# Input stages of a four-block pair-map kernel: every tile in four equal rounds, transposes first, longer leads

## The reference

```python
xn = layer_norm(x_gn)                                  # over the 64 channels of a token
left  = (xn @ Wl + bl) * sigmoid(xn @ Wlg + blg)       # block 3: times the mask too
right = (xn @ Wr + br) * sigmoid(xn @ Wrg + brg)
gate  = sigmoid(xn @ Wg + bg)
out   = einsum('kjd,kid->ijd', left, right)            # over a token axis, per channel
x     = x + (layer_norm(out) @ Wo + bo) * gate
```

## Time and profile before

| | |
|---|---|
| runs | 1729.84, 1731.24, 1733.73 us |
| profiled execution | 1738.9 us, span 1737.1 us |
| input stage of block 0 | about 51 to 223 us from the span's start |
| of block 1 | about 433 to 603 us |
| of block 3 | about 1357 to 1552 us |
| PE, DVE, ACT, POOL busy over the span | 74%, 78%, 66%, 55% |
| granted PE clock, mean | 0.916 of full speed |

### The profile page before, as it was taken

The page is one execution under the profiler, slowest core; times in us unless marked ns, Lnnn a source line. Parts: engine busy times, 40 slices in busy tenths (PEclk is TensorE's granted clock), DMA queues, the critical chain, the costliest instruction groups (busy, mean ns, idle before and its releaser), DMA issues.

```text
span 1737.1 us, 30472 instructions
## 1 busy us (share of the span) xinstructions
PE 1292.9 (74%) x9640; PEld 788.4 (45%) x9640; DVE 1361.7 (78%) x3807; ACT 1146.5 (66%) x2644; POOL 953.0 (55%) x663
## 2 busy tenths in 40 slices
PE   0588878998688887987999466677666577769665
PEld 0233366654333476654876133333334233338654
DVE  6888724997888616987999899999997777751688
ACT  0588824995788715985343577777774488851698
POOL 0799702875999504874555034444445787820454
PEclk9999998999899998998999569988998799999679
DMA  7244363776455454774443144544445334443477
GB/s 262 79 118 120 92 150 89 223 213 168 98 119 122 92 134 125 229 202 121 109 111 87 22 92 100 118 99 105 115 98 134 91 98 108 100 103 93 160 241 254
DMA packets 408784, 225.51 MB, mean 130 GB/s; under 512 B 343408, under 2 KB 343728, under 8 KB 408624
## 3 DMA queue, kind: packets, MB, share of 16 engines
q1 hardware_dynamic: 270192, 185.81, 39.3%
q10 hardware_dynamic: 138432, 37.76, 9.3%
HBM read 114.97 MB, written 66.06 MB: 104 GB/s over the span
## 4 chain that ended last, share of the span: by engine, by line
issue 29%; POOL 21%; DVE 20%; ACT 17%; PE 12%; DMA 2%; SPq 0%; POOLq 0%; ACTq 0%; DVEq 0%
ACT work L1045 12%; POOL ln_s L507 6%; DVE stats L760 5%; POOL work L499 5%; POOL work L513 4%; PE ps L1165 4%; PE ps L1282 4%; POOL work L477 3%; POOL pairs L545 2%; PE ps L1194 2%; DVE pairs L818 2%; ACT work L1058 2%; DVE stats L844 2%; ACT work L1027 1%; DVE pairs L891 1%
## 5 line engine op out<-in xcount | busy, mean ns | idle before, releaser
L507 POOL TENSOR_TENSOR ln_s<-ln_s,half_power 128x8 f32<-128x8 f32 x216 | 356.5, 1650 | 285.9 <-DVE ln_s L769 230.2
L1207 PE MATMUL ps<-wfold,work 64*128 64x320 f32 x1728 | 341.0, 486 | 100.1 <-DVE pairs L818 52.5
L1045 ACT ACTIVATE work<-work,ln_s 128x64 f32<-128x64 f32 x576 | 212.3, 429 | 116.6 <-DVE ln_s L776 116.5
L1165 PE MATMUL ps<-work,ones 128*128 128x512 f32 x432 | 241.4, 672 | 47.6 <-ACT work L1015 46.6
L1045 ACT ACTIVATE work<-pairs,ln_s 128x64 f32<-128x64 f32 x648 | 262.4, 488 | 18.9 <-DVE ln_s L776 18.9
L1207 PEld LDWEIGHTS ps<-wfold,work 64*128 64x128 f32 x1728 | 137.9, 188 | 271.9 <-DVE pairs L818 133.3
L818 DVE TENSOR_TENSOR pairs<-ps,work 128x256 f32<-128x256 f32 x288 | 169.0, 597 | 63.4 <-ACT work L1058 58.4
L1058 ACT ACTIVATE work<-ps 128x384 f32<-128x384 f32 x432 | 194.6, 476 | 4.8 <-PE ps L1207 3.8
L1194 PE MATMUL ps<-ident,work 128*128 128x128 f32 x864 | 149.1, 300 | 46.3 <-DVE work L787 26.4
L1027 ACT ACTIVATE work<-ps 128x512 f32<-128x512 f32 x216 | 128.4, 594 | 73.3 <-PE ps L1194 71.9
L1105 ACT ACTIVATE pairs<-pairs,rescale 128x256 f32<-128x256 f32 x288 | 122.4, 497 | 70.7 <-DVE work L949 70.7
(11 more groups left out here) (153 smaller groups left out, 2482.5 us busy)
## 6 DMA issues: line engine op xcount, KB each, us to landing
work<-x_mid SPq DMA_DIRECT2D x144, 256.0 KB, 2.8
gate_dram<-work ACTq DMA_DIRECT2D x108, 256.0 KB, 2.8
work<-gate_dram SPq DMA_DIRECT2D x108, 256.0 KB, 3.1
work<-in_x_in SPq DMA_DIRECT2D x72, 256.0 KB, 2.8
work<-x_nat SPq DMA_DIRECT2D x144, 128.0 KB, 2.9
x_mid<-work SPq DMA_DIRECT2D x72, 256.0 KB, 2.6
pairs<-in_x_in SPq DMA_DIRECT2D x4, 2304.0 KB, 19.3
work<-pairs SPq DMA_DIRECT2D x96, 96.0 KB, 3.0
```

The lines of the kernel that those rows point to most:

```text
L507: pool.tensor_tensor(ln_s[:, b, RSTD, :], ln_s[:, b, VAR, :], half_power[:, 0:U], ALU.pow)\
L1045: last = act.activation(dst[:, r % dst.shape[1], u * C:(u + 1) * C], src, ACT.Identity, scale=ln_s[:, b, RSTD, u:u + 1], bias=ln_s[:, b, S ...
L1165: last = pe.matmul(ps[:, bank, :], ones[:], src[:, b, :], start=first, stop=end, skip_group_check=True)
L1207: last = pe.matmul(ps[:, PAIR_BANKS[n % 3] + odd, 0:PROJ], xnT[rows, b, pair * P:(pair + 1) * P], wfold[rows, q, 0:PROJ], start=True, stop ...
```

## The change

It touches the lists of the input stages, the buffers that longer leads need, and the indices that follow from them:

- **PE** transposes tile t+1 ahead of the four projections of tile t, not between the second and the third.
- **ACT** evacuates t+1 first, then gate 0, the DMA issue, and its tokens in three parts instead of two halves, each between two gates. In blocks 0 and 1 the parts have 1, 2 and 2 tokens, in block 3 2, 2 and 2.
- **DVE** starts with shift t+2 and variance t+3, then two moments of t+4 (before: t+3), store 0, two moments, store 1, the first token of t+2, store 2, the other tokens (2, in block 3 one), store 3.
- **POOL** scales t+5 and centres t+6 (before t+4 and t+5); the power stays at t+3.
- `normed` holds six tiles, `stats` and `ln_s` hold four; the waits that guard them look as much farther back. These waits are shared with the output stages. Input and output stages get a transposed buffer each (`xnT_in`, `xnT_out`) at other addresses.
- Block 3 reads the mask straight from `mask_sb`: the copy L808 and its wait are gone, 36 of each.
- In block 0's multiplication, DVE waits for the gate stores before it writes `fold_ein`.

```diff
+NORM_RING = 6
-        normed = part(work, 1024, ROW, RING)
+        xin, normed = part(work, 0, ROW), part(work, 1024, ROW, NORM_RING)
+        xn, xnT_in = (part(work, 4096 + 1024 * k, ROW) for k in range(2))
-        stats = sb("stats", [P, 2, PAIRS, 6])
-        ln_s = sb("ln_s", [P, 2, 3, U])
+        stats = sb("stats", [P, RING, PAIRS, 6])
+        ln_s = sb("ln_s", [P, RING, 3, U])
...
 # POOL, centre
-                wait_free(pool, xn_ready, tr_base(l, 0) + t - 3)
-                wait_free(pool, xn_act, tr_base(l, 0) + t - 3)
+                if t >= NORM_RING:
+                    pool.wait_ge(xn_ready, tr_base(l, 0) + t - NORM_RING + 1)
+                    pool.wait_ge(xn_act, tr_base(l, 0) + t - NORM_RING + 1)
...
 # POOL, token_rstd (xn_ready too), and DVE, ln_shift
-                wait_free(pool, xn_act, n - 1)
+                wait_free(pool, xn_act, n - 3)
...
-                    pipeline(pool, [(4, lambda t, b, r: scale(l, t, b, r), RING),
-                                    (5, lambda t, b, r: centre(l, t, b, r), RING),
+                    pipeline(pool, [(5, lambda t, b: scale(l, t, b)),
+                                    (6, lambda t, b: centre(l, t, b)),
                                     (3, lambda t, b: token_rstd(l, 0, t, b))])
...
 # DVE, store_pair
-                if l == 3 and pair == 0:
-                    dve.tensor_copy(mask_t[:, b, :], mask_sb[:, cols(t)]).then_inc(mask_ready, 1)
-                    dve.wait_ge(mask_ready, t + 1)
...
-                    pipeline(dve, [(3, lambda t, b, r: ln_moments(l, 0, t, b, r), RING),
-                                   (0, lambda t, b: store_pair(l, 0, t, b)),
-                                   (2, lambda t, b: ln_shift(l, 0, t, b)),
-                                   (3, lambda t, b: ln_var(l, 0, t, b)),
-                                   (0, lambda t, b: store_pair(l, 1, t, b)),
-                                   (2, lambda t, b, r: normalise(l, 0, xn, t, b, r), RING),
-                                   (0, lambda t, b: store_pair(l, 2, t, b)),
-                                   (0, lambda t, b: store_pair(l, 3, t, b))])
+                    moments = lambda which: (4, lambda t, b, r: ln_moments(l, 0, t, b, r, which), RING)
+                    scaled_tokens = lambda part_: (2, lambda t, b, r: normalise(l, 0, xn, t, b, r, part_), RING)
+                    store = lambda pair: (0, lambda t, b: store_pair(l, pair, t, b))
+                    pipeline(dve, [(2, lambda t, b: ln_shift(l, 0, t, b)), (3, lambda t, b: ln_var(l, 0, t, b)),
+                                   moments((0, 1)), store(0),
+                                   moments((2, 3)), store(1),
+                                   scaled_tokens(0), store(2),
+                                   scaled_tokens(1), store(3)])
...
-                    pipeline(act, [(0, lambda t, b: gates(q, 0, t, b)),
-                                   (-1, lambda t, b: store_gate(q, t, b)),
-                                   (1, lambda t, b: evacuate_xnT(tr_base(l, 0) + t, t, b, proj_ready, PAIRS * (TILES * q + t - 1))),
-                                   (0, lambda t, b: gates(q, 1, t, b)),
-                                   (2, lambda t, b, r: normalise(l, 0, xn, xn_transposed(0), t, b, r, HALF_ONE), RING),
-                                   (0, lambda t, b: gates(q, 2, t, b)),
-                                   (2, lambda t, b, r: normalise(l, 0, xn, xn_transposed(0), t, b, r, HALF_TWO), RING),
-                                   (0, lambda t, b: gates(q, 3, t, b))])
+                    third = lambda k: (2, lambda t, b, r: normalise(l, 0, xn, xn_transposed(0), t, b, r, k, 3), RING)
+                    gate_of = lambda pair: (0, lambda t, b: gates(q, pair, t, b))
+                    pipeline(act, [(1, lambda t, b: evacuate_xnT(xnT_in, tr_base(l, 0) + t, t, b, proj_ready, PAIRS * (TILES * q + t - 1))),
+                                   gate_of(0), (-1, lambda t, b: store_gate(q, t, b)),
+                                   third(0), gate_of(1),
+                                   third(1), gate_of(2),
+                                   third(2), gate_of(3)])
...
-                    pipeline(pe, [(0, lambda t, b: project(l, 0, t, b)),
-                                  (0, lambda t, b: project(l, 1, t, b)),
-                                  (1, lambda t, b, r: transpose_xn(l, 0, t, b, r), RING),
-                                  (0, lambda t, b: project(l, 2, t, b)),
-                                  (0, lambda t, b: project(l, 3, t, b))])
+                    projected = lambda pair: (0, lambda t, b: project(l, pair, t, b))
+                    pipeline(pe, [(1, lambda t, b, r: transpose_xn(l, 0, t, b, r), RING),
+                                  projected(0), projected(1), projected(2), projected(3)])
```

More of the change, by code:

```diff
@@ L123, in part @@
             return buf[:, lo:lo + n * bufs].rearrange("p (b f) -> p b f", b=bufs)
-        xin, _, _, xn, xnT = (part(work, 1024 * k, ROW) for k in range(5))
-        normed = part(work, 1024, ROW, RING)
+        xin, normed = part(work, 0, ROW), part(work, 1024, ROW, NORM_RING)
+        xn, xnT_in = (part(work, 4096 + 1024 * k, ROW) for k in range(2))
         sig = part(work, 6144, U * 3 * C)
@@ L136, in build @@
         xres, gate = part(work, 0, ROW, RING), part(work, 8192, ROW, RING)
-        xn_out = part(work, 2048, ROW, RING)
+        xn_out, xnT_out = part(work, 2048, ROW, RING), part(work, 4096, ROW)
         xnew, shifted, squares = (part(work, 5120 + 1024 * k, ROW) for k in range(3))
@@ L250, in build @@
          in_moments, in_step, in_summed,
-         s_apart) = [sem(f"sem_{k}") for k in range(83)]
+         s_apart) = [sem(f"sem_{k}") for k in range(82)]
         x_loaded, gate_stored, xnew_stored, mres_loaded, qT_ready, hqT_ready = [
@@ L754, in output_weights, with ln_moments, small @@
                 last.then_inc(w_step, 1)
[L756 to L757 removed]
+            def ln_moments(l, side, t, b, r, which=range(PAIRS)):
+                if side == 0 and which[0] == 0:
                     dve.wait_ge(x_scaled, input_base(l) + t + 1)
[L759 to L764 removed]
+                for k in which:
+                    last = dve.bn_stats(stats[:, t % RING, k, :], ln_pair(side, t, r, k))
+                if which[-1] == PAIRS - 1:
+                    last.then_inc(ln_step, 1)
+            def small(t, k):
+                return ln_s[:, t % RING, k, :]
             def ln_var(l, side, t, b):
                 dve.wait_ge(ln_step, tr_base(l, side) + t + 1)
[L769 removed]
+                dve.tensor_scalar(small(t, VAR), of_stats(t, 2), C * LN_EPS, None, ALU.add).then_inc(var_ready, 1)
             def ln_shift(l, side, t, b):
@@ L979, in _ @@
                         move_products(q, k)
+                        if l == 0 and k == 2:
+                            for b in range(2):
+                                dve.wait_ge(gate_stored[b], 8 * TILES)
                         if l == 0 and k in (2, 4):
@@ L1038, in normalise @@
                 first = DVE_TOKENS[l, side]
-                middle = (first + U) // 2
-                for u in range(first if 0 in halves else middle, U if 1 in halves else middle):
+                bound = lambda k: first + (U - first) * k // parts
+                for u in range(bound(part_), bound(part_ + 1)):
                     if side == 0:
-                        src = normed[:, r, u * C:(u + 1) * C]
+                        src = normed[:, t % NORM_RING, u * C:(u + 1) * C]
                     else:
@@ L1206, in project @@
                     rows = slice(C * odd, C * odd + C)
-                    last = pe.matmul(ps[:, PAIR_BANKS[n % 3] + odd, 0:PROJ], xnT[rows, b, pair * P:(pair + 1) * P],
+                    last = pe.matmul(ps[:, PAIR_BANKS[n % 3] + odd, 0:PROJ], xnT_in[rows, b, pair * P:(pair + 1) * P],
                                      wfold[rows, q, 0:PROJ], start=True, stop=True)
```

75 lines of the change are left out of this document (33 added, 42 removed).

## The result

The changed kernel takes **1853.7 us** (median of four runs, 1852.6 to 1854.8). The kernel before, run beside it, takes 1730.5. The ratio is 1.0695, 95% interval 1.0667 to 1.0722. The forecast was 1804 with a range up to 1842: the direction was right and the size was not. The kernel before was run again beside every group of runs, on other chips too, and its median lies between 1730.5 and 1739.4; so small differences between groups are read from the ratios, and not from the times.

What follows compares the result with a forecast made beforehand. The prediction took an ACT-DVE loop as the bound, 4.42 us a tile (block 3: 5.15). New loops and prologues add 26 us each in blocks 0 and 1, 21 in block 3: +73, median 1804, range 1764 to 1842.

Steps and rivals of the forecast that it cites:

- The old loop: Input stages before the change: ACT and DVE run a loop by turns, 4.42 us a tile, which the change cuts.
- Loop A: Input stages: transposes through ACT's evacuation, gates and tokens to DVE's last tokens and the next transposes, 4.93 us a tile.
- the sum: All input stages: 26 us more for each of blocks 0 and 1, 21 for block 3, +73 in all.
- Loop B: Input stages: DVE's variance, POOL's power and passes, then DVE tokens held by those passes, 5.05 us a tile.
- the gap: Between POOL's two passes, where DVE's first token can start; rival: block 3 catches it, 5.17 a tile, 1788 us, chance 0.25.
- the miss: Block 3: DVE's first token is held to the end of POOL's second pass in every tile, 5.75 us a tile.
- The clock: Rival: PE's clock falls, transposes and projection 0 slow, 1.2 us more for a third of 108 tiles, 1844 us, chance 0.19.
- their 26: Blocks 0 and 1, each stage: 19.1 us from 29 tiles, 3.1 from the last 6, prologue 4.5, less about 0.7.
- Costed at nothing: Mask copy, SP's loads, gate stores, output stages, block 0's multiplication wait and block 2's statistics index were given no cost.
- the mask copy: Block 3: its removal, 36 x 0.2 us on DVE, was costed at nothing because DVE waits anyway.
- The lock of the Trainium skill: Shared DVE and POOL port: a DVE token would hold POOL 0.22 to 0.30 us a tile, sum about 14 us higher.

Runs made afterwards that it cites:

- f1: Changed kernel with POOL's two input-stage passes cut to 8 elements and four extra PE matmuls a tile behind projection 3: 1786.0 us, ratio 1.0289.
- e3: Changed kernel with PE's transposes back between projections 1 and 2 and ACT's evacuation behind gate 0 and the DMA issue: 1769.4 us, ratio 1.0213.
- g1: Changed kernel with the gates' store issued behind gate 3 and four extra PE matmuls a tile behind projection 3: 1810.8 us, ratio 1.0423.
- h1: Changed kernel with four extra PE matmuls a tile and a small multiplication added on POOL in every tile: 1826.6 us, ratio 1.0516.
- e1: Changed kernel with four extra PE matmuls a tile behind projection 3, their result unused: 1847.0 us, ratio 1.0655.
- g2: Changed kernel with only the gates' store moved, issued behind gate 3 of its own tile: 1829.8 us, ratio 1.0536.
- e2: Changed kernel with POOL's centring and scaling passes in the input stages cut to 8 elements: 1798.5 us, ratio 1.0382.
- f3: Kernel before the change with only block 3's mask copy and its wait removed, mask read in place: 1725.5 us, ratio 0.9945.
- b1: Changed kernel's buffers, leads and mask with new PE, ACT and DVE orders, and variance and POOL's power at t+4: 1695.1 us, ratio 0.9769.
- f2: Changed kernel with short POOL passes, four extra PE matmuls a tile, and the gates' store issued behind gate 3: 1758.6 us, ratio 1.0125.

## Why the forecast was right, and where it failed

**The old loop** was cut as said: between 80 and 206 us ACT never waits for a shift at its tokens, and idles 3.5 us before them in all. In the kernel before it waited 5.3 us for shifts there.

**Loop A**, 4.93 forecast, 5.07 measured (f1). By its steps from the transposes at 108.75: gate 0 at 1.53 and not 1.41 (projection 0 started at 0.59 and not 0.55; 0.13 passed from its end to the gate, not 0.05); next ACT instruction 0.64 and not 0.59 later; gate 1 at 2.52, gate 2 at 3.55, store 2 at 4.06; the last tokens at 4.50. Where nothing holds them they take 0.51, are done at 5.01, and the next transposes come at 5.07, as in f1. The loop was right and its distances 0.14 short. As 5.08 was taken for a tile, that cost the sum nothing by itself; what it did was to make DVE's first token late.

**Loop B**, 5.05 forecast, 5.04 measured in blocks 0 and 1 (e3). Held DVE tokens, the power behind the variance and the passes behind the power are all in the rows.

**The sentence that failed** is "The two loops share store 3 and the last tokens, so I take 5.08 for blocks 0 and 1". 5.08 is near what a tile that catches the gap takes: 5.22 behind a slow tile in the change, 5.07 in g1, where the issue is elsewhere, and 5.23 in h1 with 0.16 more on POOL. But I asked for the gap in block 3 alone. In blocks 0 and 1 the first token wants to start at 3.48 (117.45 less 113.97), and POOL's second pass starts at 3.47. By the forecast's own steps it was 2.34 + 0.51 + 0.46 = 3.31 against some 3.7, a margin of 0.4, and it was never worked out; Loop A's 0.17 more and a scaling pass that ended 0.2 earlier used it up. A missed tile is 5.68 (e1), 0.6 more. In block 3 I took the miss, and 5.75 was near the 5.66 of e1. That was in part luck: I had the margin at 0.1 and could not tell its side, and it is 0.37.

**The clock** is the second term that failed: the sum has it at nothing, and 0.895 was granted over block 0's tiles. It was the rival with 0.19: a third of the tiles, 1.2 each, 1844 us. That is what the trace has in blocks 0 and 1: one tile of three, 1.07 over the 5.08. What speaks against the rival as I put it is e1: the full clock alone gives back 7 us and not 40, since each tile then misses the gap. With the gap caught (g2 to g1) it gives 19, without passes (e2 to f1) 12.5. The forecast had the two as separate cases and never a case in which both come. Either alone keeps the tiles long: 5.68 with the gap missed at full clock (e1), 5.45 with the gap caught and the clock falling (g2, where g1 has 5.07). Whether a held token brings the slow clock on is open. In blocks 0 and 1 of the change the slow tile follows PE's idle time of 2.18, but the clock falls in e2 too, where no token is held. In the slow tile the token comes only when the second pass is ending, and the tile after it is in the gap again.

**The sum.** By the tiles' means, blocks 0 and 1: 29 tiles x (5.69 - 5.08) = 18 a stage, of the 19 and 21 that the stages are over their 26. Block 3: 28 x (5.92 - 5.75) = 5 of the 9; the rest lies in its first and last tiles and wasn't taken apart. Together the stages have 48 of the 50 us by which 1804 was short, and the tiles named here some 40 of them.

**Costed at nothing.** The reason given for the mask copy was wrong: its 0.21 a tile was in the old loop of block 3 (f3), where I had called it work of a DVE that waits. It cost the sum nothing, since the sum took the old tile of 5.15 as measured and built the new ones without the copy. By itself the edit was worth some 7 us to the kernel before. Loads, gate stores and the output stages are not seen to cost anything: the input stages hold 121 of the 123 us.

**The lock of the Trainium skill** ("SBUF — State Buffer", "Who interferes with whom"), by which POOL would be held in turn and the sum 14 us higher: DVE is held, as in the earlier trace rows. POOL isn't held for a token's 0.3, as far as the rows tell. In g1, with a token in the gap, the second pass starts 1.23 behind the first (121.97 to 123.20) as it does in e1 (122.04 to 123.27), and takes 1.31 and not 1.27. Beside POOL's power of 1.64 DVE isn't held either: three tokens take 0.76 in b1.

**Left open:** what decides in which tile the clock falls; what makes the first two or three tiles of a stage 6 us and longer in some runs, and b1's slow tiles of block 0.

## What to carry to other kernels

Where engines share one loop, an order that cuts it can close others: write down every loop of the new order with its length, and for each instruction that another engine can hold, the margin to the moment at which it is held. A margin of a few hundredths of a microsecond is then a result to be distrusted, since every tile lands on the same side of it. And price a slow clock and a held instruction together: here each alone kept the tiles long, so that taking away only one gained little.

## What was unexpected of the hardware

- Adding 0.2 us of work a tile to POOL made the kernel some 20 us faster (e1 to h1: 20 by the times, 24 by the ratios), by moving its passes 0.16 past the moment at which a DVE token arrives.
- One missed start costs a whole POOL pass: a token of 0.29 takes 1.23 to 1.29 once POOL's pass has started 0.01 to 0.10 ahead of it (117.44 and 117.45 in the changed kernel).
- The granted clock went down for one tile in three of block 0, in step with the pattern: after PE had idled 2.17 us the transposes took 1.12 us, after 1.54 and 1.71 they took 0.66. But the idle time just before doesn't decide it: 1.12 came behind 1.70 in g2 and 1.11 behind 1.55 in e2, and in block 3 of the change 0.65 behind 2.32:

```profile
1493.96 0.65 PE L1194 MATMUL ps<-ident,work 128*128 128x128 f32 x4 [2.32 <-DVE work L789]
```

- A DMA issue on ACT's queue costs 0.27 us where the instruction behind it is on the path (f1 to f2), though no row of ACT shows it as busy.
